# Two layers of attention and experts on one core: opening vectors on VectorE, key sums two steps later, layer 1's first loads ahead of the boundary

## What is computed

```python
x = L0_attn_x
xn = _layernorm(x)
s = _L0_attn_ref(xn, ...)          # recurrence over 256 tokens, 8 heads of 16
g = _silu(_L0_ffn_ref(xn, ...))    # 64 experts of width 64, 8 chosen from 4 of 8 groups, + shared expert
x = x + s * g
xn = _layernorm(x)
s = _L1_attn_ref(xn, ...)          # causal attention, 16 heads of 8, rotary q and k
g = _silu(_L1_ffn_ref(xn, ...))    # 16 experts of width 256, 3 chosen
x = x + s * g
```

## Time and profile before

| what | us |
|---|---|
| median of 3 runs | 2169.27 (2168.54 to 2169.32) |
| the profiled execution | 2166.51 |
| its span, first to last instruction | 2164.8 |
| busy in the span: PE, DVE, ACT, POOL | 1634.9, 1583.1, 1134.5, 1019.8 |
| layer 0 with its opening | to about 1190 |
| layer 1 | from 1191.5 |

### The profile page before, as it was taken

The page is one execution under the profiler, slowest core; times in us unless marked ns, Lnnn a source line. Parts: engine busy times, 40 slices in busy tenths (PEclk is TensorE's granted clock), DMA queues, the critical chain, the costliest instruction groups (busy, mean ns, idle before and its releaser), DMA issues. The chain is left out here.

```text
span 2164.8 us, 32713 instructions
## 1 busy us (share of the span) xinstructions
PE 1634.9 (76%) x8418; PEld 1187.9 (55%) x8418; DVE 1583.1 (73%) x4335; ACT 1134.5 (52%) x1811; POOL 1019.8 (47%) x1114
## 2 busy tenths in 40 slices
PE   3186786886858758597684299898999988878876
PEld 2154454554535535364452298787888865555554
DVE  3199989999999999999998444444444457667763
ACT  1265464664636646366453154544545546666664
POOL 2766877677777867777795000000000003323332
PEclk8598888898988979789898599999999989999997
DMA  4410020110200102002000511001110000000000
GB/s 85 100 40 15 1 65 1 28 38 1 64 0 21 43 1 64 0 11 48 1 10 10 126 21 25 19 13 26 21 25 10 16 25 16 15 15 15 22 15 13
DMA packets 140675, 58.82 MB, mean 27 GB/s; under 512 B 94711, under 2 KB 135148, under 8 KB 140524
## 3 DMA queue, kind: packets, MB, share of 16 engines
q1 hardware_dynamic: 140524, 57.19, 11.8%
HBM read 36.05 MB, written 21.10 MB: 26 GB/s over the span
## 5 line engine op out<-in xcount | busy, mean ns | idle before, releaser
L594 PE MATMUL pb<-hid,wd 128*128 128x512 f32 x528 | 301.4, 656 | 192.0 <-POOL hid L406 191.1
L402 POOL TENSOR_TENSOR hid<-act_g,act_u 128x512 f32<-128x512 f32 x256 | 328.2, 1282 | 163.5 <-ACT act_c L518 148.3
L518 ACT ACTIVATE act_g<-pb 128x512 f32<-128x512 f32 (+1 forms) x264 | 158.1, 599 | 371.2 <-PE pb L545 329.6
L406 POOL TENSOR_TENSOR hid<-hid,act_c 128x512 f32<-128x512 f32 x256 | 328.7, 1284 | 21.5 <-POOL hid L402 1.8
L1762 DVE SCALAR_TENSOR_TENSOR l_acc<-l_pb,l_gtok,l_acc 128x128 f32<-128x128 f32 x512 | 144.4, 344 | 257.0 <-PE l_pb L1406 256.7
L1321 ACT ACTIVATE l_hid<-l_pb,l_cols 128x512 f32<-128x512 f32 x256 | 169.4, 688 | 183.1 <-PE l_pb L1406 182.7
L543 PE MATMUL pb<-xt_hi,wg_hi 128*128 128x512 f32 (+1 forms) x264 | 190.3, 721 | 91.3 <-ACT act_g L518 91.3
L1406 PEld LDWEIGHTS l_pb<-l_big,l_hid 128*128 128x128 f32 x2048 | 247.1, 192 | 10.6
L1406 PE MATMUL l_pb<-l_big,l_hid 128*128 128x128 f32 x2048 | 247.9, 275 | 0.0
L1406 PE MATMUL l_pb<-l_xt,l_big 128*128 128x512 f32 x768 | 219.1, 420 | 26.5 <-DVE l_rope L1694 24.9
L594 PEld LDWEIGHTS pb<-hid,wd 128*128 128x128 f32 x528 | 101.7, 206 | 246.5 <-POOL hid L406 220.1
(11 more groups left out here) (314 smaller groups left out, 3881.6 us busy)
## 6 DMA issues: line engine op xcount, KB each, us to landing
z_scratch<-zs SPq DMA_DIRECT2D x128, 81.0 KB, 3.0
zr<-z_scratch SPq DMA_DIRECT2D x8, 1296.0 KB, 8.1
x_sb<-in_L_attn_x_dram SPq DMA_DIRECT2D x32, 64.0 KB, 2.1
g_scratch<-zs SPq DMA_DIRECT2D x8, 256.0 KB, 2.8
y_scratch<-yo SPq DMA_DIRECT2D x8, 256.0 KB, 2.1
l_xs<-in_L_attn_x_dram SPq DMA_DIRECT2D x32, 64.0 KB, 1.9
l_ys<-y_scratch SPq DMA_DIRECT2D x128, 16.0 KB, 1.8
l_gs<-g_scratch SPq DMA_DIRECT2D x8, 256.0 KB, 3.0
```

The costliest lines, as they stand in the source:

```text
L402: pool.tensor_tensor(hid1[:, :], g, u, ALU.mult).then_inc(s_h1, 1)
L406: pool.tensor_tensor(hid[:, (p + par) % 2, :], hid1[:, :], c, ALU.mult).then_inc(s_h, 1)
L518: act.activation(dst, pb[0:n, what, :], ACT.Silu if what == 0 else ACT.Copy).then_inc(s_ev, 1)
L594: last = pe.matmul(pb[:, SUM, :], wd[0:n, p, :], hid[0:n, (p + par) % 2, :], start=(p == 0), stop=(p == PAIRS), skip_group_check=True)
```

## The change

- Opening: `products(0, 0)` and `vectors(0, 0)` move from POOL to DVE. POOL waits, ahead of its chunk 3, for all 14 of DVE's results.
- Layer 0's loop: `key_sums` at step 22, the key norm's root at slot 81, `vectors` before pair 29. Layer norm and routing have one small DVE instruction less each; the layer norm's centring is a scalar_tensor_tensor.
- Boundary: layer 1's buffers for weights and tile 0 now lie in layer 0's `wg_hi`, `wg_lo`, `wd` and ring buffers, and are filled as soon as the last expert product has been taken (`s_dn`). SP issues W1 in four quarters, the 22 weights and tile 0's loads ahead of the last y store. POOL zeroes five buffers and splits W1 ahead of `gated(NT - 1, 1)`. In layer 1 only W2 is left to load first, POOL zeroes two buffers, and DVE no longer splits W1.

```diff
-        LN, PREP, POST, ROUTE = 3, 7, 4, 58
+        LN, PREP, POST, ROUTE = 2, 7, 4, 57
-        LN_AT, ROUTE_AT = {(0, 0): 0, (0, 1): 1, (1, 0): 2, (3, 0): 3, (4, 0): 4, (4, 1): 5, (6, 1): 6}, 11
-        POST_AT, SUM_AT, COEF_AT = (10, 13), 20, 24
-        NORM_SLOT, INPUT_SLOT, POST_SLOT, KEY_SLOT = 12, 60, 39, 78
-        POST_PAIRS, PREP_PAIRS = (7, 17), (21, 28)
+        LN_AT, ROUTE_AT = {(0, 0): 0, (1, 0): 1, (3, 0): 2, (4, 0): 3, (4, 1): 4, (6, 1): 5}, 11
+        POST_AT, SUM_AT, COEF_AT = (10, 13), 22, 24
+        NORM_SLOT, INPUT_SLOT, POST_SLOT, KEY_SLOT = 12, 60, 39, 81
+        POST_PAIRS, PREP_PAIRS = (7, 17), (21, 29)
...
@@ sync, end of layer 0
             tile(NT - 1, 1, False, False, False)
+            store_gate(NT - 1)
...
+            sp.wait_ge(s_dn, NT * (PAIRS + 1))
+            w1 = area.w1.rearrange("p (e f) -> p e f", e=E1)
+            for i in range(4):
+                at = slice(i * (E1 // 4), (i + 1) * (E1 // 4))
+                sp.dma_start(w1[:, at, :], d["L1_ffn_W1"][at].rearrange("e i f -> i e f")).then_inc(area.s_w1[i], 16)
+            w(area.ident, d["c_ident"])
...
+            sp.wait_ge(area.s_init, ZEROED)
+            w(area.rows[0:2 * E1, :], d["L1_ffn_b1"].rearrange("e (a p) -> (e a) p", a=2))
...
+            sp.wait_ge(s_yst, 16)
+            sp.wait_ge(s_gst, 16)
+            load_tile(sp, d, (y_dram, g_dram), area, 0)
             store_y(NT - 1)
-            store_gate(NT - 1)
@@ gpsimd, layer 0
                 if k == 3:
-                    products(0, 0)
-                    vectors(0, 0)
+                    pool.wait_ge(s_pq, WHOLE)
...
             tile(NT - 1, 1, False, False)
+
+            pool.wait_ge(s_dn, NT * (PAIRS + 1))
+            for buffer in (area.rows, area.wkv, area.b2, area.wv, area.bo):
+                pool.memset(buffer, 0.0).then_inc(area.s_init, 1)
+            for i in range(4):
+                at = slice(i * (E1 * F1 // 4), (i + 1) * (E1 * F1 // 4))
+                pool.wait_ge(area.s_w1[i], 16)
+                pool.tensor_scalar(area.w1_hi[:, at], area.w1[:, at], 1.0, 1.0, ALU.mult, ALU.mult).then_inc(area.s_w1h, 1)
+                pool.wait_ge(area.s_w1h, i + 1)
+                pool.tensor_tensor(area.w1_lo[:, at], area.w1[:, at], area.w1_hi[:, at].bitcast(F32), ALU.subtract).then_inc(area.s_w1s, 1)
             gated(NT - 1, 1)
             normed(NT - 1)
@@ vector, layer 0
-                    dve.tensor_scalar(x_mean, x_sum, -1.0 / D, None, ALU.mult).then_inc(s_ln, 1)
-                elif stage == 2:
-                    dve.wait_ge(s_ln, t * LN + 2)
-                    dve.tensor_tensor(xc[:, :, :], x_sb[:, :, :], over(x_mean, D), ALU.add).then_inc(s_xc, 1)
+                    dve.scalar_tensor_tensor(out=xc[:, :, :], in0=over(x_sum, D), scalar=-1.0 / D, in1=x_sb[:, :, :],
+                                             op0=ALU.mult, op1=ALU.add).then_inc(s_xc, 1)
...
-                    dve.tensor_scalar(cw_sum, cw_sum, 1e-20, None, ALU.add).then_inc(s_rt, 1)
+                    dve.tensor_scalar(cw_sum, cw_sum, 1e-20, 1.0 / ROUTE_SCALE, ALU.add, ALU.mult).then_inc(s_rt, 1)
...
             for stage in range(STAGES):
                 route(0, stage)
+            q, k, f, p, g, am = (field(0, at) for at in (ZQ, ZK, ZF, ZP, ZG, ZA))
+            dve.wait_ge(s_sig, 1)
+            dve.wait_ge(s_silu, 1)
+            dve.tensor_tensor(am, f, k, ALU.mult).then_inc(s_pq, 1)
...
             key_sums(0, 0)
+            dve.tensor_tensor(p, q, f, ALU.mult).then_inc(s_pq, 1)
             for stage in range(6):
                 coefficients(0, 0, stage)
+            dve.wait_ge(s_pr, PREP)
+            dve.tensor_tensor(k, k, wide(root, HD0), ALU.mult).then_inc(s_pq, 1)
...
+            dve.wait_ge(s_pq, RAW + 8)
+            dve.tensor_tensor(p, p, prod[:, :, :], ALU.add).then_inc(s_pq, 1)
             tile(0, 0, True, True)
@@ gpsimd, layer 1
-            zeroed = rows[:, :], wkv[:, :], b2[:, :], wv[:, :], bo[:, :], ones[:, :], gT[:, :]
-            for i, (buffer, value) in enumerate((*((z, 0.0) for z in zeroed), (eps[:, 0:1], LN_EPS), (ones[0:1, :], 1.0))):
+            for i, (buffer, value) in enumerate(((ones[:, :], 0.0), (gT[:, :], 0.0), (eps[:, 0:1], LN_EPS), (ones[0:1, :], 1.0))):
@@ vector, layer 1
             route(0, 0)
-            for i, ready in enumerate((s_w1, s_w1b)):
-                dve.wait_ge(ready, 16)
...
-                dve.tensor_copy(w1_hi[:, at], src).then_inc(s_w1s, 1)
-                dve.wait_ge(s_w1s, 2 * i + 1)
-                dve.tensor_tensor(w1_lo[:, at], src, w1_hi[:, at].bitcast(F32), ALU.subtract).then_inc(s_w1s, 1)
```

More of the change, by code:

```diff
@@ L58, in check, with __init__, sb, carve @@
         assert self.n == self.per_tile, (self.n, self.per_tile)
-def layer0(nc, d, scratch, sem):
+class Shared:
+    RING = 3
+    def __init__(self, nc, ctx, sem):
+        def sb(name, shape, dt=F32):
+            return ctx.enter_context(nc.sbuf_tensor("shared_" + name, shape, dt))
+        self.wg_hi, self.wg_lo = (sb(name, [P, (E0 + 1) * F0], F32R) for name in ("hi", "lo"))
+        self.wd = sb("down", [P, PAIRS + 1, D])
+        self.rings = sb("rings", [P, 3 * self.RING * TOK])
+        self.place = 0
+        self.ident, self.rot, self.wo0, self.wkv, self.b2, self.wv, self.wo, self.bo, self.mask = (self.carve(P) for _ in range(9))
+        self.rows = self.carve(P)[0:2 * E1 + 4]
+        self.cosT, self.sinT = self.carve(N), self.carve(N)
+        self.wproj = self.carve(2 * D).rearrange("p (j c) -> p j c", j=2)
+        self.xs, self.ys, self.gs = (self.carve(NS * D).rearrange("p (s c) -> p s c", s=NS) for _ in range(3))
+        self.gate, self.qmask, self.kspare = self.carve(E1), self.carve(4), self.carve(1)
+        self.w1_hi, self.w1_lo = self.wg_hi[:, 0:E1 * F1], self.wg_lo[:, 0:E1 * F1]
+        self.w1 = self.wd[:, :, :].rearrange("p a n -> p (a n)")[:, 0:E1 * F1]
+        self.s_init = sem("m_constants_set")
+        self.s_w = sem("m_weights_loaded")
+        self.s_w1 = [sem(f"m_w1_loaded{i}") for i in range(4)]
+        self.s_w1h = sem("m_w1_hi_written")
+        self.s_w1s = sem("m_w1_split")
+        self.s_x = sem("m_x_loaded")
+        self.s_yld = sem("m_y_loaded")
+        self.s_gld = sem("m_gate_loaded")
+    def carve(self, n):
+        self.place += n
+        assert self.place <= 3 * self.RING * TOK
+        return self.rings[:, self.place - n:self.place]
@@ L63, in layer0 @@
+def layer0(nc, d, scratch, sem, area):
     z_dram, y_dram, g_dram = scratch
@@ L890, in tile @@
                     step(t, par, n, first, ahead)
-            for stage in range(7):
+            for stage in range(6):
                 layer_norm(0, 0, stage)
@@ L1148, in _ @@
[L1148 to L1160 removed]
+            def load(t):
+                load_tile(sp, d, (y_dram, g_dram), area, t)
```

178 lines of the change are left out of this document (80 added, 98 removed).

## The result

The changed kernel takes 2133.36 us (median of 4 runs, 2126.22 to 2134.53) where the kernel before takes 2168.90 (2167.75 to 2169.32): a ratio of 0.983, 95% interval 0.981 to 0.985. That is faster, as predicted, but by 35.5 us rather than 58. The time lies above the predicted range. The profiled execution took 2133.49, 33.0 less than that of before, with a span of 2131.8.

What follows compares the result with a forecast made beforehand. VectorE's recurrence was taken to bound layer 0's loop, and POOL the opening. Gains of 7.8 (opening), 25.9 (loop) and 24.2 (boundary) sum to 57.9 us, from 2169.3 to a median of 2111.4, range 2102 to 2124.

Steps and rivals of the forecast that it cites:

- Opening: Start to first step: first tile's products and vectors on VectorE rather than POOL save 7.8 us.
- the wait for `raws`: Layer 0's loop: VectorE's wait for POOL's last product ahead of the key sums goes in six tiles, 26.1 us.
- the new wait for the key root: Layer 0's loop: VectorE newly waits for ACT's later key-norm root, 1.5 us in all.
- rival 1: Layer 0's loop: table loads stay before ACT's root, so VectorE waits 12 to 13 us; 2122 us, chance 0.13.
- Dropped instructions: Layer 0's loop: fewer small routing and layer norm instructions save 0.2 us a tile, 1.3 over seven.
- What is late next?: Layer 0's loop without the `raws` wait: ACT's root costs 1.5 us of new waits; POOL's vectors tie with the coefficients.
- the out-norm waits: Layer 0's loop: VectorE's waits for the root of the output norm stay at 3.8 us.
- Boundary, W1: End of layer 0: loading and splitting W1 ahead of POOL's `gated` delays it by 2.3 us.
- Boundary, the weights: Start of layer 1: with the 22 weights already loaded, VectorE starts 1.25 us in rather than 20.95, saving 19.7.
- Layer 1: From the first rotary operation to the end nothing changes, 0 us gain.
- rival 4: Layer 1 gets a lower TensorE clock and the kernel is slower than before, 2189 us; chance 0.03.
- rival 5: Layer 0's side takes up the loads' gain, layer 1 isn't brought forward, only opening and loop count; 2136 us, chance 0.04.

Runs made afterwards that it cites:

- e11: Kernel before the change with only the first tile's key products and vectors moved to VectorE; 2158.66 us, ratio .996.
- e2: Changed kernel with the key sums that feed the coefficients, and minus beta, in PSUM instead of SBUF; 2111.44 us, ratio .976.
- e7: e2 with key sums, key root and POOL's vectors back at the places of the kernel before; 2134.31 us, ratio .984.
- e6: Changed kernel with VectorE's reciprocal of the output norm behind step 14 instead of 13; 2126.93 us, ratio .981.
- e8: Changed kernel with the edits of e2, e5 and e6 together; 2109.96 us, ratio .973.
- e10: e2 with the output norm's reciprocal behind step 14 instead of 13 and the coefficients from step 25 instead of 24; 2108.77 us, ratio .974.
- e3: Changed kernel with POOL's memset of the row of ones held back until VectorE has split layer 1's small weights; 2123.33 us, ratio .980.
- after: The changed kernel itself, against the kernel before; 2133.36 us, ratio .983.
- e5: Changed kernel with two of W1's four splits and the row-of-ones memset held back behind layer 1's weight preparation; 2125.49 us, ratio .981.

## Why the prediction was wrong

The forecast missed by 24.9 us of the profiled execution: 17.0 in the loop, 6.8 at the boundary, 1.5 behind it, less 0.5 in the opening.

**Opening: right.** 8.3 for 7.8, chunk 3, ACT's start and the vectors each within 0.4 us, and e11 shows that it carries through. The later kernels, with a gain of 9.1 to 10.3 at the first step, have the earlier load of `zr` on top.

**Loop, the wait for `raws`: right.** 26.1 gone as worked out, the new wait for the key root 0.5 where I had 1.5; rival 1 didn't come. Dropped instructions 0.9 (1.3).

**Loop, the failed step: "What is late next?"** I went on through ACT's root and POOL's vectors and took DVE's coefficients at their durations of before: the sum has no term for them. The same rows had both halves of the answer: the coefficient products are two-operand operations, and POOL's 6.60 us of idleness stood right beside them. The change removes that idleness (2.51 is left, at the end), so the three products ahead of it run beside expert products. It costs 12.8 us (11.9 on these three, 0.9 on `neg_beta`), and e2 and e7 show it. Worse, the opening's paragraph of the prediction has the rule and a row for it (L692, 2.72 us), applied to the vectors and to the recurrence's steps, but not to the `between` work.

The Trainium skill (SBUF — State Buffer, Who interferes with whom) says that a VectorE instruction with two SBUF inputs contends with a GpSimd instruction that reads SBUF, that the loser blocks fully, and that one with at most one SBUF input outside the 2-port modes doesn't. The rows agree: 1.10 and 1.13 us, ending 0.05 and 0.06 behind POOL's, against 0.18 with an operand in PSUM.

**Loop, the out-norm waits: mis-sized.** I had 3.8 staying; they were 8.6, and in kernels with the same loop 4.9 and 3.9. Part is spread; what the rest is isn't shown. It hangs together with ACT's order: e6 and e8 show such waits return at ACT's next root, e10 that moving DVE's side of both removes them. The loop's 17.0 are then 12.8 for the coefficients, 4.8 for these waits, 0.4 for the dropped instructions, less 1.0 for the key root.

**Boundary, W1: mechanism right, term mis-sized.** 2.3 became 6.6. The expert side ended at E - 15.9 rather than E - 19 (3.1): I had it move a pair earlier against DVE, and it moved 0.9 later (E - 16.8 before); which of its waits did that isn't shown; the gate store and first issue took 2.9 rather than 2 (0.9); landing took 4.7 rather than 4.3 (0.4). The splits took 3.44 each as said. Of the 6.6, about 0.9 came back in a shorter way from store to layer 1.

**Boundary, the weights: right** (19.65 for 19.7), **but the row of ones was costed at nothing.** I counted four constants as "left" and never placed the fifth, 3.51 us (L1280), which the early splits set free. It cost 3.3 us on DVE's first cast; e3 removes them. Together: 24.2 - 4.3 + 0.9 - 3.3 = 17.5 against 17.4.

**Layer 1: right.** 924.5 for 923.0; rival 4 didn't come: the mean granted clock from the rotary operation to the end is 0.96 in both kernels. The time lies near rival 5's 2136, but its mechanism is refuted: layer 1 was brought forward by 17.4 us at the boundary.

## What to carry to other kernels

When a change removes an engine's idle time, ask what had been running undisturbed beside it: list VectorE's two-operand and cast operations in that stretch with the place of each operand, and read their durations at a spot where GpSimd is busy, not where it waits. If such a two-operand operation can't be moved, put one operand into PSUM: here that took the products to 0.18 to 0.19 us in every tile. A prepared boundary has more than one bound: with half of the splits gone SP's queue was late next, and a loop made faster brings the end of the side work, and with it all prefetches, later against its own end.

## What was not expected of the hardware

- A POOL memset, which reads nothing, held up a VectorE cast (3.55 us instead of 0.23) and a `tensor_scalar` on 128x4 elements (2.29 instead of 0.17), but not a `tensor_tensor` with both operands in SBUF: in the kernel before L1694 took its 0.69 inside the memset that lasts from 1241.98 to 1245.49:

```profile
1243.21 0.69 DVE L1694 TENSOR_TENSOR l_rope<-l_rope 128x512 f32<-128x512 f32 x1
```

- A 128x4 operation of 0.17 us pays as much for a collision as one of 512 elements: the wait has the length of what is left of POOL's instruction, not of its own.
- Profiled executions of kernels with the same loop (after, e3, e5) differ by 4.7 us in its waits for the output root (3.9 to 8.6), and the changed kernel's four runs by 8.3 in all. The four of the kernel before beside them lie within 1.6, but its runs in the later comparisons spread over 3.0 to 5.8, and e3's over 2.3: one execution alone can't carry a difference of 5 us.
